# Splitting VectorE's long two-operand operations into instructions of 256 elements, in a graph-network layer

## The chip, the cores and the metric

One NeuronCore of one Trainium2 chip runs the program. The metric is the device time of one execution in microseconds (us); lower is better. The kernel before takes 764.09 us (median of 3 runs, 762.74 to 765.07).

## The reference, cut to what matters

The layer has 50,000 nodes and 25,000 edges (sorted by target node), with rows of 64 floats. Each edge gets an attention score from its type's weight matrix; a softmax over the edges of one target weighs the source rows; then two small products, a leaky ReLU of each, a residual and a layer norm.

```python
proj = jnp.einsum('ni,rio->nro', nfeat, relation_weight)      # 10 relations, 64x64 each
att = jnp.sum(proj[src, etype] * jnp.tanh(proj[dst, etype] + efeat), axis=-1)
ex = jnp.exp(att - segment_max(att, dst)[dst])
a = ex / segment_sum(ex, dst)[dst]
h_nb = segment_sum(nfeat[src] * a[:, None], dst)
out = leaky_relu((nfeat + h_nb) @ res_fc_w.T, 0.01) + leaky_relu(nfeat * h_nb @ res_fc2_w.T, 0.01)
x = layernorm(x + out)
```

Nodes without an incoming edge have h_nb = 0. So the kernel computes every node as if it had none (the "dense" work, 49 tiles of 1,024 nodes), and then overwrites the rows of the nodes that have edges.

## The kernel before, in words

**Edge steps.** Each of the 128 partitions holds 196 consecutive edges (T = 196). A step `s` takes 8 of these columns (COLS = 8, NS = 25 steps, the last of 4 columns). The program of each compute engine is one loop over s = -1 to 28. In it stand the main work of step s (ten relations: VectorE masks, TensorE multiplies), the softmax sums of step s-1 (called e), the head, product and leaky ReLU of step s-2 (called f), the layer norm of step s-3 (called l), and three dense tiles as long as there are any: the last of the 49 is in step 15.

**The rows in and out.** GpSimd (POOL in the profile) issues indirect DMAs only: 384 gathers of x rows into `xsd` (line 441; 128 rows each, indices read from `ends_i`), then 196 scatters of `out_r` into `out` (line 465; indices from `row_i`), and two for the edges that cross partitions: a gather of `es_end` from `hist` ahead of the last 28 scatters, and the very last one. The numbers 0 to 383 below are the gathers, 384 is the first scatter.

**The pace.** So that the gathers don't all come at once, GpSimd waits ahead of its n-th DMA for a point of TensorE's program: as many TensorE instructions (matmuls and weight loads, behind the 12 of the setup) as n*14.6 - 250 for the gathers and n*13.64 - 82 for the scatters. The functions `pe_marks` and `pace` find the semaphore and value for it:

```python
PACE, LEAD, PACE_OUT, LEAD_OUT = 14.6, 250, 13.64, 82
need = [k for k, (_, _, work) in enumerate(marks) if work <= min(n * PACE - LEAD if n < G_MOVES[NS] else n * PACE_OUT - LEAD_OUT, step_end)]
```

A scatter of step s waits also for `fmul_done`, the gather of `es_end` for the store of `hist`.

**What the change touches.** All of it is on VectorE (DVE): `dense_centre` (line 984: zd <- zsd, zd, once for a dense tile), `pair` (lines 1004 and 1005: uw <- h_t, xsd; the sum and the product of head and x), `leaky` (line 1011: l12 in place), `final_add` (1016), `final_add_x` (1021) and `final_centre` (1032), once a step each. All read two tensors from SBUF. `pair_turn` of TensorE and `heads` of ScalarE wait for `uw_done`. Beside these VectorE runs the masks (`xm`, line 912, ten a step, one operand in PSUM), reductions (lines 979, 989, 1026, 1039) and short sums (954).

**The end.** In step 26 VectorE waits at line 1167 for `es_end`; ScalarE's `fmul_done` of the last steps comes behind that.

Of the kernel before, what the change touches and what calls it, by code (L numbers as in the profile page):

```python
# [5 lines left out]
ALU = mybir.AluOpType  # L6
# [6 lines left out]
P = 128  # L13
DMA = 16
COLS = 8
QUAD = 4
BIG = 3.0e38
NONE = 1.0e30
FAR = 1 << 20
SLOPE = 0.01  # L20
EPS = 1e-5

RX = 13
# [11 lines left out]
def wait(eng, sem, value):  # L35

    if value > 0:
        eng.wait_ge(sem, value)


def gnn_resnorm(nc, x, src, dst, eattr, etype, relw, resw, resw2, out):
    N, D = x.shape
# [4 lines left out]
    DR = 512 // D  # L47
# [5 lines left out]
    A0 = (P - 1) // DMA * DMA  # L53
    assert D == 64 and T % QUAD == 0 and (N - (ND - 1) * DB) % DR == 0 and 0 < LASTC < T and T - LASTC <= E

    def cols(s):
        return min(COLS, T - s * COLS)

    def groups(s):
        return cols(s) // QUAD  # L60

    G_BEFORE = [0]
    for s in range(NS):
        G_BEFORE.append(G_BEFORE[-1] + groups(s))
    Q_BEFORE = [2 * n for n in G_BEFORE]
    C_BEFORE = [QUAD * n for n in G_BEFORE]

# [28 lines left out]
    with ExitStack() as ctx:  # L96
# [9 lines left out]
        def sems(name, n):  # L106
# [31 lines left out]
        xsd = sb("xsd", [P, RX, COLS, 2, D])  # L138
# [15 lines left out]
        zsd = sb("zsd", [P, DR])  # L154
# [4 lines left out]
        h_t = sb("h_t", [P, COLS, D])  # L159
        uw = sb("uw", [P, COLS, 2, D])  # L160
        uwT = sb("uwT", [P, 2, 512])
        l12 = sb("l12", [P, COLS, 2, D])
        zf = sb("zf", [P, COLS, D])
        zs = sb("zs", [P, COLS])
        zcf = sb("zcf", [P, 2, COLS, D])
# [37 lines left out]
        zadd_done, zsum_done, zmid_done, dsq_done, dred_done = (  # L203
            sem("zadd_done"), sem("zsum_done"), sem("zmid_done"), sem("dsq_done"), sem("dred_done"))
        sqrt_done, rec_done, dmul_done = sem("sqrt_done"), sem("rec_done"), sem("dmul_done")
        h_done, uw_done, y12_done, pf_done = sem("h_done"), sem("uw_done"), sem("y12_done"), sem("pf_done")
        l_done, z1_done, z2_done, fsum_done, fsub_done = sem("l_done"), sem("z1_done"), sem("z2_done"), sem("fsum_done"), sem("fsub_done")
# [282 lines left out]
        def _(pe):  # L490
# [71 lines left out]
                mm.then_inc(y_done, 1)  # L562

            def pair_turn(f, g):
                pe.wait_ge(uw_done, f + 1)
                wait(pe, tr_out, TR_PAIR[f, g])
                for j in range(QUAD):
                    mm = pe.transpose(tr_ps[:, j * P:(j + 1) * P], uw[:, g * QUAD + j, :, :].rearrange("p k f -> p (k f)"),  # L568
                                      ident[:, :])
                mm.then_inc(tr_in, 1)  # L570
# [13 lines left out]
            for s in range(-1, LAST + 1):  # L584
                main, e, f = 0 <= s < NS, s - 1, s - 2
# [75 lines left out]
        def _(act):  # L661
# [44 lines left out]

            def heads(f, g):
                act.wait_ge(frec_done, f + 1)
                wait(act, uw_done, f)
                for j in range(g * QUAD, (g + 1) * QUAD):  # L710
                    ins = act.activation(h_t[:, j, :], es[:, f % RS, j, :], ACT.Copy, scale=rs[:, f % 2, j:j + 1])  # L711
                ins.then_inc(h_done, 1)
# [34 lines left out]
            for s in range(-1, LAST + 1):  # L747
                e, f, l, o = s - 1, s - 2, s - 3, s - 4
# [79 lines left out]
        def _(v):  # L828
# [152 lines left out]
            def dense_centre(d):  # L981
                v.wait_ge(zsum_done, d + 1)
                z = zd[:, d % RZ, :].rearrange("p (j f) -> p j f", f=D)
                v.scalar_tensor_tensor(z, zsd[:, :].unsqueeze(2).to_broadcast([P, DR, D]), -1.0 / D, z, ALU.mult, ALU.add).then_inc(zmid_done, 1)  # L984

            def dense_sum(d):
                v.wait_ge(dsq_done, d + 1)
# [8 lines left out]
                v.reciprocal(rstd[:, s % 2, :, :], sd[:, s % 2, :, :]).then_inc(rec_done, 1)  # L996

            def pair(f):
                n = cols(f)
                xd = xsd[:, f % RX, 0:n, 1, :]  # L1000
                v.wait_ge(h_done, G_BEFORE[f + 1])
                if f > 0:
                    v.wait_ge(tr_in, TR_PAIR[f - 1, groups(f - 1) - 1] + 1)
                v.tensor_tensor(uw[:, 0:n, 0, :], h_t[:, 0:n, :], xd, ALU.add)
                v.tensor_tensor(uw[:, 0:n, 1, :], h_t[:, 0:n, :], xd, ALU.mult).then_inc(uw_done, 1)

            def leaky(f):
                n = cols(f)
                v.wait_ge(pf_done, Q_BEFORE[f + 1])
                l = l12[:, 0:n, :, :].rearrange("p j k f -> p (j k f)")  # L1010
                v.scalar_tensor_tensor(l, l, SLOPE, l, ALU.mult, ALU.max).then_inc(l_done, 1)

            def final_add(f):
                n = cols(f)
                v.wait_ge(l_done, f + 1)
                v.tensor_tensor(zf[:, 0:n, :], l12[:, 0:n, 0, :], l12[:, 0:n, 1, :], ALU.add).then_inc(z1_done, 1)

            def final_add_x(f):
                n = cols(f)
                v.wait_ge(z1_done, f + 1)  # L1020
                v.tensor_tensor(zf[:, 0:n, :], zf[:, 0:n, :], xsd[:, f % RX, 0:n, 1, :], ALU.add).then_inc(z2_done, 1)

            def final_sum(f):
                n = cols(f)
# [3 lines left out]
            def final_centre(f):  # L1028
                n = cols(f)
                v.wait_ge(fsum_done, f + 1)  # L1030
                wait(v, fmul_done, f - 1)
                v.scalar_tensor_tensor(zcf[:, f % 2, 0:n, :], zs[:, 0:n].unsqueeze(2).to_broadcast([P, n, D]), -1.0 / D,
                                       zf[:, 0:n, :], ALU.mult, ALU.add).then_inc(fsub_done, 1)

            def final_squares(f):
                n = cols(f)
# [5 lines left out]
            for s in range(-1, LAST + 1):  # L1042
                main, e, f, l = 0 <= s < NS, s - 1, s - 2, s - 3
# [169 lines left out]
```

## Time and profile before

| | |
|---|---|
| median of 3 runs | 764.09 us (762.74 to 765.07) |
| profiled execution, span | 764.9 us (its own time is this span, first to last instruction; 0.1% above the median) |
| busy | PE 556.2 (73%), DVE 634.8 (83%), ACT 499.1 (65%), POOL 581.8 (76%) |
| instructions | DVE 1115, POOL 590 |
| chain that ended last | POOL, with line 465 |
| TensorE clock granted | 0.917 in the mean |

POOL's busy time counts each DMA instruction's descriptor work and not the pause behind it, so 76% does not say by itself whether the engine ever waits. DVE's busy share of 83% is a mean over a long stretch of nearly full use and a tail with little to do.

### The profile page before, as it was taken

To read this page: it belongs to the slowest core of one execution; us is meant where nothing else is said; L and a number is where in the kernel's file an instruction comes from. 1 tells how busy PE (TensorE), PEld (TensorE's weight loads), DVE (VectorE), ACT (ScalarE), POOL (GpSimd) and SP (SyncE) were. 2 spreads that over 40 slices of the span, in tenths; PEclk is the share of its full clock that TensorE was granted. 3 is DMA by queue.
4 is the path that set the end of the run, shared out by engine and by line. 5 is a ranking of instruction groups with operands and counts; after the bars stand their busy time and mean duration, and the time that the engine had idled before them with its cause. 6 is when DMAs were issued, how large, how long until landed. Compare 5 with 4: busy or idle time off the path is not lost. (4 is left out here: it accounts for less than half of the span.)

```text
span 764.9 us, 14665 instructions
## 1 busy us (share of the span) xinstructions
PE 556.2 (73%) x3780; PEld 293.9 (38%) x3780; DVE 634.8 (83%) x1115; ACT 499.1 (65%) x1474; POOL 581.8 (76%) x590
## 2 busy tenths in 40 slices
PE   1887888888789788888889887788888788632000
PEld 0652454445345345345345343333333333321000
DVE  1689999999999999999999999999999899742010
ACT  0366677679778779779778777765656446755040
POOL 6777777777777777777777777777777777777776
PEclk9999999999999999999999999999999999755555
DMA  5463435434434434434444332422112221000000
GB/s 134 105 191 81 124 89 144 124 87 145 124 95 137 125 106 126 133 106 117 138 107 115 104 104 73 108 73 75 48 46 74 75 83 44 28 26 17 19 18 16
DMA packets 49457, 70.41 MB, mean 92 GB/s; under 512 B 17450, under 2 KB 20966, under 8 KB 49374
## 3 DMA queue, kind: packets, MB, share of 16 engines
q1 hardware_dynamic: 30750, 52.33, 21.2%
q0 software_dynamic: 18624, 17.16, 10.9%
q8 instruction: 30, 0.49, 0.3%
q14 instruction: 53, 0.43, 0.2%
HBM read 45.61 MB, written 25.78 MB: 93 GB/s over the span
## 5 line engine op out<-in xcount | busy, mean ns | idle before, releaser
L441 POOL DMA_INDIRECT xsd<-in_x,ends_i x384 | 378.2, 985 | 118.0 <-issue 108.6
L543 PE MATMUL t_ps<-xm,w_rel 64*64 64x512 f32 (+1 forms) x1000 | 270.3, 622 | 39.7 <-DVE xm L912 39.2
L912 DVE SCALAR_TENSOR_TENSOR xm<-typ,xT_ps 128x1024 f32<-128x1024 f32 (+1 forms) x250 | 292.4, 1187 | 2.6 <-issue 2.6
L545 PE MATMUL h_ps<-xm,w_rel 64*64 64x512 f32 (+1 forms) x1000 | 270.2, 622 | 0.0
L465 POOL DMA_INDIRECT out<-out_r,row_i x196 | 200.6, 1023 | 59.7 <-issue 55.5
L560 PE MATMUL y_ps<-bd_cat,dT 128*128 128x256 f32 x392 | 97.9, 394 | 17.6 <-DVE zd L974 14.8
L691 ACT ACTIVATE o_t<-zd,rstd 128x64 f32<-128x64 f32 x392 | 98.8, 337 | 14.9 <-DVE rstd L996 14.9
L543 PEld LDWEIGHTS t_ps<-xm,w_rel 64*64 64x64 f32 x1000 | 52.7, 135 | 142.7 <-DVE xm L912 117.4
L578 PE MATMUL s_ps<-bd_both,uwT 128*128 128x128 f32 x392 | 73.4, 313 | 36.6 <-issue 35.9
L578 PEld LDWEIGHTS s_ps<-bd_both,uwT 128*128 128x128 f32 x392 | 54.9, 203 | 115.1 <-issue 95.3
L560 PEld LDWEIGHTS y_ps<-bd_cat,dT 128*128 128x128 f32 x392 | 72.5, 195 | 30.9 <-issue 12.8
L954 DVE SCALAR_TENSOR_TENSOR es<-es,wd,wx 128x64 f32<-128x64 f32 x196 | 55.7, 284 | 11.7 <-ACT wx L704 0.6
L698 ACT ACTIVATE wd<-delta 128x16 f32<-128x16 f32 (+1 forms) x25 | 5.4, 216 | 88.7 <-DVE delta L942 84.4
L568 PE MATMUL tr_ps<-ident,uw 128*128 128x128 f32 x196 | 34.4, 302 | 27.0 <-ACT uwT L718 15.6
L723 ACT COPY l<-s_ps 128x256 f32<-128x256 f32 x98 | 35.2, 359 | 26.9 <-PE s_ps L578 26.9
L545 PEld LDWEIGHTS h_ps<-xm,w_rel 64*64 64x64 f32 x1000 | 52.7, 135 | 0.0
L704 ACT ACTIVATE wx<-xsd,wd 128x64 f32<-128x64 f32 x196 | 52.1, 337 | 0.8
L711 ACT ACTIVATE h_t<-es,rs 128x64 f32<-128x64 f32 x196 | 49.4, 337 | 0.0
L743 ACT ACTIVATE out_r<-zcf,rstd 128x64 f32<-128x64 f32 x196 | 49.2, 333 | 0.1
L568 PEld LDWEIGHTS tr_ps<-ident,uw 128*128 128x128 f32 x196 | 22.3, 150 | 66.8 <-issue 35.0
L974 DVE TENSOR_TENSOR zd<-rd,y_ps 128x512 f32<-128x512 f32 x49 | 33.4, 682 | 9.2 <-ACT rd L677 9.2
L684 ACT ACTIVATE sqd<-zd 128x512 f32<-128x512 f32 x49 | 30.9, 631 | 12.7 <-DVE zd L984 12.6
(143 smaller groups left out, 742.1 us busy)
## 6 DMA issues: line engine op xcount, KB each, us to landing
xsd<-in_x SPq DMA_DIRECT2D x1024, 0.2 KB
x_in<-in_x SPq DMA_DIRECT2D x48, 256.0 KB
typ<-typ_d SPq DMA_DIRECT2D x24, 512.0 KB
out<-o_t SPq DMA_DIRECT2D x48, 256.0 KB
xsd<-in_x,ends_i POOLq DMA_INDIRECT x384
hist<-es SPq DMA_DIRECT2D x24, 256.0 KB, 2.0
ea<-in_edge_attr SPq DMA_DIRECT2D x24, 224.0 KB
out<-out_r,row_i POOLq DMA_INDIRECT x196, 2.1
```

The costliest lines, as they stand in the source:

```text
L441: pool.indirect_dma_start(xsd[:, s % RX, j, side, :], None, x[:, :], bass.IndirectOffsetOnAxis(ap=ends_i[:, side, c:c + 1], axis=0),).then ...
L465: pool.indirect_dma_start(out[:, :], bass.IndirectOffsetOnAxis(ap=row_i[:, c:c + 1], axis=0), out_r[:, s % RW, j, :], None, bounds_check=t ...
L543: pe.matmul(t_ps[h * D:(h + 1) * D, 0:n], w_rel[0:D, r, :], xm[0:D, b, h * n:(h + 1) * n], start=(r == 0), stop=(r == R - 1), skip_group_c ...
L545: mm = pe.matmul(h_ps[(1 - h) * D:(2 - h) * D, 0:n], w_rel[D:P, r, :], xm[D:P, b, (1 - h) * n:(2 - h) * n], start=False, stop=(r == R - 1) ...
L560: mm = pe.matmul(y_ps[:, j * 2 * P:(j + 1) * 2 * P], dT[:, d % 2, j * P:(j + 1) * P], bd_cat.rearrange("p k f -> p (k f)"), start=True, st ...
L568: mm = pe.transpose(tr_ps[:, j * P:(j + 1) * P], uw[:, g * QUAD + j, :, :].rearrange("p k f -> p (k f)"), ident[:, :])
L578: mm = pe.matmul(s_ps[:, YQ + j * P:YQ + (j + 1) * P], uwT[:, q // 2, k * P:(k + 1) * P], bd_both[:, :], start=True, stop=True)
L691: ins = act.activation(o_t[:, d % RO, j * D:(j + 1) * D], zd[:, d % RZ, j * D:(j + 1) * D], ACT.Copy, scale=rstd[:, s % 2, d % 3, j:j + 1])
L704: ins = act.activation(wx[:, j, :], xsd[:, e % RX, j, 0, :], ACT.Copy, scale=wd[:, e % 2, 0, j:j + 1])
L711: ins = act.activation(h_t[:, j, :], es[:, f % RS, j, :], ACT.Copy, scale=rs[:, f % 2, j:j + 1])
L912: v.scalar_tensor_tensor(xm[:, (s * R + r) % RM, 0:n], typ[:, s % RT, 0:n], float(r), xT_ps[:, 0:n], ALU.is_equal, ALU.mult).then_inc(mask ...
L954: v.scalar_tensor_tensor(es[:, e % RS, j, :], old, wd[:, e % 2, 1, j:j + 1], wx[:, j, :], ALU.mult, ALU.add).then_inc(chain_done, 1)
```

## The change

The operations named above are cut along their columns into instructions of 4 columns (256 elements), or 2 columns of `l12` (2 x 2 x 64 = 256 elements). `leaky` becomes four instructions, the others two each. All but `pair` wait and signal as before (the last piece signals). `pair` runs group by group: it waits for `h_done` of 4 columns, adds and multiplies them, and signals `uw_done` once per group; `pair_turn` and `heads` count `uw_done` in groups.

```diff
+HALF = 4
             def pair_turn(f, g):
-                pe.wait_ge(uw_done, f + 1)
+                pe.wait_ge(uw_done, G_BEFORE[f] + g + 1)
...
             def heads(f, g):
-                wait(act, uw_done, f)
+                wait(act, uw_done, G_BEFORE[f])
...
             def dense_centre(d):
-                v.scalar_tensor_tensor(z, zsd[:, :].unsqueeze(2).to_broadcast([P, DR, D]), -1.0 / D, z, ALU.mult, ALU.add).then_inc(zmid_done, 1)
+                for j in range(0, DR, HALF):
+                    ins = v.scalar_tensor_tensor(z[:, j:j + HALF, :], zsd[:, j:j + HALF].unsqueeze(2).to_broadcast([P, HALF, D]), -1.0 / D,
+                                                 z[:, j:j + HALF, :], ALU.mult, ALU.add)
+                ins.then_inc(zmid_done, 1)
...
             def pair(f):
-                n = cols(f)
-                xd = xsd[:, f % RX, 0:n, 1, :]
-                v.wait_ge(h_done, G_BEFORE[f + 1])
                 if f > 0:
                     v.wait_ge(tr_in, TR_PAIR[f - 1, groups(f - 1) - 1] + 1)
-                v.tensor_tensor(uw[:, 0:n, 0, :], h_t[:, 0:n, :], xd, ALU.add)
-                v.tensor_tensor(uw[:, 0:n, 1, :], h_t[:, 0:n, :], xd, ALU.mult).then_inc(uw_done, 1)
+                for g in range(groups(f)):
+                    j = slice(g * QUAD, (g + 1) * QUAD)
+                    xd = xsd[:, f % RX, j, 1, :]
+                    v.wait_ge(h_done, G_BEFORE[f] + g + 1)
+                    v.tensor_tensor(uw[:, j, 0, :], h_t[:, j, :], xd, ALU.add)
+                    v.tensor_tensor(uw[:, j, 1, :], h_t[:, j, :], xd, ALU.mult).then_inc(uw_done, 1)
...
             def leaky(f):
-                l = l12[:, 0:n, :, :].rearrange("p j k f -> p (j k f)")
-                v.scalar_tensor_tensor(l, l, SLOPE, l, ALU.mult, ALU.max).then_inc(l_done, 1)
+                for j in range(0, n, 2):
+                    l = l12[:, j:j + 2, :, :].rearrange("p j k f -> p (j k f)")
+                    ins = v.scalar_tensor_tensor(l, l, SLOPE, l, ALU.mult, ALU.max)
+                ins.then_inc(l_done, 1)
...
             def final_add(f):
-                v.tensor_tensor(zf[:, 0:n, :], l12[:, 0:n, 0, :], l12[:, 0:n, 1, :], ALU.add).then_inc(z1_done, 1)
+                for j in range(0, n, QUAD):
+                    ins = v.tensor_tensor(zf[:, j:j + QUAD, :], l12[:, j:j + QUAD, 0, :], l12[:, j:j + QUAD, 1, :], ALU.add)
+                ins.then_inc(z1_done, 1)
```

`final_add_x` and `final_centre` are cut in the same way as `final_add`.

VectorE's program in the middle of one step, before, from the last small score operation to the first mask behind `pair` (line 942 is `restarts`, 912 `mask`):

```order
L942 TENSOR_TENSOR delta<-delta,start 128x8 [waits sub_done]
L1004 TENSOR_TENSOR uw<-h_t,xsd 128x8x64 [waits tr_in,h_done]
L1005 TENSOR_TENSOR uw<-h_t,xsd 128x8x64
L984 SCALAR_TENSOR_TENSOR zd<-zsd,zd 128x512 [waits zsum_done]
L912 SCALAR_TENSOR_TENSOR xm<-typ,xT_ps 128x1024 [waits quad_done] x2
```

The same place in the changed program (its line numbers are up to 13 higher):

```order
L943 TENSOR_TENSOR delta<-delta,start 128x8 [waits sub_done]
L1009 TENSOR_TENSOR uw<-h_t,xsd 128x4x64 [waits h_done,tr_in]
L1010 TENSOR_TENSOR uw<-h_t,xsd 128x4x64
L1009 TENSOR_TENSOR uw<-h_t,xsd 128x4x64 [waits h_done]
L1010 TENSOR_TENSOR uw<-h_t,xsd 128x4x64
L986 SCALAR_TENSOR_TENSOR zd<-zsd,zd 128x256 [waits zsum_done]
L986 SCALAR_TENSOR_TENSOR zd<-zsd,zd 128x256
L913 SCALAR_TENSOR_TENSOR xm<-typ,xT_ps 128x1024 [waits quad_done] x2
```

Three instructions between the score work and the next mask have become six; the mask keeps its place behind them, and the first half of `uw` is whole after two of them.

VectorE's program at the end of the same step, before:

```order
L969 RECIPROCAL rs<-s_all 128x8 [waits h_done,den_done]
L1011 SCALAR_TENSOR_TENSOR l<-l 128x1024 [waits pf_done]
L1016 TENSOR_TENSOR zf<-l 128x512 [waits l_done]
L919 TENSOR_TENSOR prod<-t_ps,g_t 128x512 [waits att_done,tanh_done]
L1021 TENSOR_TENSOR zf<-zf,xsd 128x512 [waits z1_done]
```

And in the changed program:

```order
L970 RECIPROCAL rs<-s_all 128x8 [waits h_done,den_done]
L1017 SCALAR_TENSOR_TENSOR l<-l 128x256 [waits pf_done]
L1017 SCALAR_TENSOR_TENSOR l<-l 128x256 x3
L1024 TENSOR_TENSOR zf<-l 128x256 [waits l_done]
L1024 TENSOR_TENSOR zf<-l 128x256
L920 TENSOR_TENSOR prod<-t_ps,g_t 128x512 [waits att_done,tanh_done]
L1031 TENSOR_TENSOR zf<-zf,xsd 128x256 [waits z1_done]
L1031 TENSOR_TENSOR zf<-zf,xsd 128x256
```

Nothing changes its place; three instructions with two SBUF operands have become eight, and `product`, which TensorE waits for, stands behind six of them instead of two. The programs of TensorE, ScalarE, GpSimd and SyncE keep their instructions and their order.

## Rows read from the trace of the kernel before

**Rows 1.** Chain that ended last, in order of time: start us, us, what.
```profile
758.85 0.30 issue
759.15 0.97 POOL out L465
```

**Rows 2.** Waits of POOL: waited for, us in total, times, longest.
```profile
POOL xsd L441 <- issue: 108.6, 356, 0.3
POOL out L465 <- issue: 55.5, 182, 0.3
POOL xsd L441 <- PE h_ps L545: 5.5, 18, 0.3
```

**Rows 3.** Lines 441 and 465: duration ns min/median/max, then first and last start.
```profile
L441 POOL DMA_INDIRECT xsd<-in_x,ends_i x384: 940/944/2074, 3.6 to 497.6; - x192
L465 POOL DMA_INDIRECT out<-out_r,row_i x196: 971/972/1947, 498.8 to 759.2; - x196
```

**Rows 4.** Page, groups: the same two lines, busy us, mean ns.
```profile
L441 POOL DMA_INDIRECT xsd<-in_x,ends_i x384 | 378.2, 985 | 118.0 <-issue 108.6
L465 POOL DMA_INDIRECT out<-out_r,row_i x196 | 200.6, 1023 | 59.7 <-issue 55.5
```

**Rows 5.** Timeline of DVE, middle of a step: start us, us, what.
```profile
311.99 0.69 DVE L1004 TENSOR_TENSOR uw<-h_t,xsd 128x512 f32<-128x512 f32 x1
312.59 0.69 DVE L1005 TENSOR_TENSOR uw<-h_t,xsd 128x512 f32<-128x512 f32 x1
313.19 0.69 DVE L984 SCALAR_TENSOR_TENSOR zd<-zsd,zd 128x512 f32<-128x512 f32 x1
```

**Rows 6.** Timeline of POOL beside it.
```profile
312.63 1.47 POOL L441 DMA_INDIRECT xsd<-in_x,ends_i  x1 [0.30 <-issue]
314.40 0.94 POOL L441 DMA_INDIRECT xsd<-in_x,ends_i  x1 [0.30 <-issue]
```

**Rows 7.** Timeline of DVE and of POOL, end of a step without dense work.
```profile
556.11 1.23 DVE L1011 SCALAR_TENSOR_TENSOR l<-l 128x1024 f32<-128x1024 f32 x1 [0.34 <-ACT l L723]
...
556.85 1.33 POOL L465 DMA_INDIRECT out<-out_r,row_i  x1 [0.30 <-PE h_ps L545]
```

**Rows 8.** Timeline of POOL and of DVE, the longest gather.
```profile
478.92 2.07 POOL L441 DMA_INDIRECT xsd<-in_x,ends_i  x1 [0.30 <-PE h_ps L545]
...
478.86 0.69 DVE L1004 TENSOR_TENSOR uw<-h_t,xsd 128x512 f32<-128x512 f32 x1
479.47 0.69 DVE L1005 TENSOR_TENSOR uw<-h_t,xsd 128x512 f32<-128x512 f32 x1
```

**Rows 9.** Timeline of DVE, the step of 4 columns: operations of 256 elements.
```profile
685.83 0.42 DVE L1004 TENSOR_TENSOR uw<-h_t,xsd 128x256 f32<-128x256 f32 x1
686.17 0.42 DVE L1005 TENSOR_TENSOR uw<-h_t,xsd 128x256 f32<-128x256 f32 x1
686.51 0.68 DVE L1026 TENSOR_REDUCE zs<-zf 128x8 f32<-128x512 f32 x1
```

**Rows 10.** Groups of DVE by form, 200 to 600 us: busy, mean ns, idle before.
```profile
L912 DVE SCALAR_TENSOR_TENSOR xm<-typ,xT_ps 128x1024 f32<-128x1024 f32 x156 | 185.9, 1209 | 0.0
...
L1011 DVE SCALAR_TENSOR_TENSOR l<-l 128x1024 f32<-128x1024 f32 x16 | 19.2, 1200 | 3.3 <-ACT l L723 3.3
```

**Rows 11.** Windows from the start: us, then busy and instructions (x) by engine.
```profile
0.00:482.60 482.60, 394.82 (x2654) 215.57 (x2654) 445.94 (x764) 355.82 (x1068) 367.05 (x380) 0.99 0.42 117
```

**Rows 12.** Timeline of POOL, the last gathers and the first scatter.
```profile
493.84 0.94 POOL L441 DMA_INDIRECT xsd<-in_x,ends_i  x1 [0.30 <-issue]
...
498.83 1.00 POOL L465 DMA_INDIRECT out<-out_r,row_i  x1 [0.30 <-issue]
```

**Rows 13.** Groups of POOL in 500:620, 620:700 and 700:765.
```profile
L465 POOL DMA_INDIRECT out<-out_r,row_i x92 | 93.0, 1011 | 28.1 <-issue 24.4 <-PE h_ps L545 3.0 <-PE s_ps L578 0.6
L465 POOL DMA_INDIRECT out<-out_r,row_i x58 | 62.4, 1076 | 17.7 <-issue 17.1 <-PE s_ps L578 0.3 <-PE h_ps L545 0.3
L465 POOL DMA_INDIRECT out<-out_r,row_i x46 | 45.1, 980 | 14.0 <-issue 14.0
```

**Rows 14.** Timeline of DVE, the wait for es_end.
```profile
725.49 0.28 DVE L1167 SCALAR_TENSOR_TENSOR before<-es_end,fix,xT_ps 128x64 f32<-128x64 f32 x1 [26.55 <-DMA es_end<-hist,fix_i]
```

More of the change, by code:

```diff
@@ L1020, in final_add_x @@
                 v.wait_ge(z1_done, f + 1)
-                v.tensor_tensor(zf[:, 0:n, :], zf[:, 0:n, :], xsd[:, f % RX, 0:n, 1, :], ALU.add).then_inc(z2_done, 1)
+                for j in range(0, n, QUAD):
+                    ins = v.tensor_tensor(zf[:, j:j + QUAD, :], zf[:, j:j + QUAD, :], xsd[:, f % RX, j:j + QUAD, 1, :], ALU.add)
+                ins.then_inc(z2_done, 1)
             def final_sum(f):
@@ L1031, in final_centre @@
                 wait(v, fmul_done, f - 1)
-                v.scalar_tensor_tensor(zcf[:, f % 2, 0:n, :], zs[:, 0:n].unsqueeze(2).to_broadcast([P, n, D]), -1.0 / D,
-                                       zf[:, 0:n, :], ALU.mult, ALU.add).then_inc(fsub_done, 1)
+                for j in range(0, n, QUAD):
+                    ins = v.scalar_tensor_tensor(zcf[:, f % 2, j:j + QUAD, :], zs[:, j:j + QUAD].unsqueeze(2).to_broadcast([P, QUAD, D]),
+                                                 -1.0 / D, zf[:, j:j + QUAD, :], ALU.mult, ALU.add)
+                ins.then_inc(fsub_done, 1)
             def final_squares(f):
```

## Prediction

> **What bounds the kernel now.** I read the chain that ended last first. It is GpSimd from end to end, in the pattern 0.30 us of issue and 0.97 us of an indirect DMA [rows 1]. The list of GpSimd's waits says that this holds for the whole span: 356 gathers and 182 scatters began 0.3 us behind the one before them with nothing to wait for, and where TensorE is named it is the same 0.3 us at most [rows 2]. So the pace is not felt today, and the time is a sum over one engine: 582 DMAs, each with a pause of 0.30 us. What can shorten it is the DMA instruction itself. Its median is 944 ns for a gather and 972 ns for a scatter, with longest ones of 2074 and 1947 [rows 3], but the means are 985 and 1023 [rows 4]. The difference is time lost on the chain: 384 x 0.041 = 15.7 us in the gathers and 196 x 0.051 = 10.0 us in the scatters, 25.7 us in all.
>
> **What lengthens a DMA instruction.** I laid the two timelines side by side. The gather of 312.63 took 1.47 us, 0.53 more than its median [rows 6]. It began while L1005 ran (312.59, 0.69 us, so to 313.28) [rows 5], and 0.53 is the time from its start to that end, less 0.12. The scatter of 556.85 is 0.36 too long, and L1011 ran from 556.11 to 557.34: 0.49 less 0.13 [rows 7]. So a DMA instruction that starts inside a VectorE operation with two SBUF operands stands until this operation ends. The masks, with one operand in PSUM, are far more numerous (L912, 156 in 400 us [rows 10]), and I found no gather held by one. The other lengthened instructions that I laid beside VectorE's timeline fit in the same way, most of them with L1005 and L1011. As a rule a GpSimd instruction gets in between two such operations in a row: that of rows 6 did, with L984 right behind L1005. Not always: the one of 478.92 started in L1004, and was held through L1005 as well, to 480.16 [rows 8].
>
> The Trainium skill, SBUF — State Buffer, section "Who interferes with whom", describes this: VectorE and GpSimd share one port pair, taken as an exclusive lock for a whole instruction, and a VectorE instruction with two SBUF inputs contends with a GpSimd one that reads SBUF. The trace agrees (0.53 us). The same section infers that a tensor_tensor does not hold back descriptor generation; L1005 is a TENSOR_TENSOR and does. What that would make of the time is the second rival.
>
> **What the pieces give.** Held at most for the rest of one operation, a DMA loses up to 0.69 - 0.13 = 0.56 us behind 512 elements and up to 1.1 behind 1024; a piece lasts 0.42 us in the record [rows 9], so at most 0.42 - 0.13 = 0.29 can be lost, on average half of that, 0.15. The chance to be hit stays, as the pieces cover the same stretch and a little more. In the scatters without dense work today's loss is 92 x (1011 - 972) = 3.6 us, then 58 x (1076 - 972) = 6.0 us, then 46 x 8 ns = 0.4 us [rows 13]. The first part is ten delays like that of rows 7, each of which would be near 0.15 on average; the second, at 104 ns for each of 58, has to hold some much longer ones, which would be at most 0.29. I take 3.6 to 1.8, 6.0 to 2.4, and 0.4 to 0.2: 4.4 us lost, 5.6 us won. If each delay were placed badly (0.29), the gain is 3; if well, 8.
>
> For the gathers the same halving would give about 8 of 15.7 us, if nothing else stopped them. The pace does.
>
> **What the pieces cost.** A step gets 8 more instructions (pair 2, leaky 3, the other three 1 each), and each of the 49 dense tiles 1: 25 x 8 + 49, about 245. The price of one more can be read: two operations of 512 elements start 0.60 us apart (311.99, 312.59, 313.19 [rows 5]), two of 256 elements 0.34 (685.83, 686.17, 686.51 [rows 9]): 2 x 0.34 - 0.60 is 0.07 to 0.08, I take 0.07. Nothing hides it on VectorE: it has no idle time ahead of its masks in 400 us, and 3.3 us ahead of sixteen L1011 [rows 10], which can swallow a little of it. So masks, and TensorE's program behind them, come 0.07 x 11 = 0.77 us later in each step with dense work, and the delays add up from step to step.
>
> This matters through the pace. GpSimd's n-th gather may not start before TensorE has done n x 14.6 - 250 instructions. For n = 380 that is 5298. The window to 482.60 has 2654 + 2654 = 5308, less 12 of the setup 5296 [rows 11], so the point is reached at about 482.6; the gather was issued at 493.84 [rows 12]. The slack is 11.2 us. By then the changed VectorE has run some 14 steps x 8 and 49 dense pieces more: 161 x 0.07 = 11.3 us. A GpSimd that ran 8 us ahead would need 19; so in the second half of the gathers GpSimd runs into the pace and follows TensorE. The first scatter (498.83 before [rows 12]) then comes at 498.83 - 11.2 + 11.3, so where it was; with some of VectorE's waits swallowed, 1 us sooner. The gain of the gathers is given back.
>
> The scatters have a laxer pace: for the first, n = 384, 384 x 13.64 - 82 = 5156 instructions, 200 less than the gathers' rule would ask, some 18 us of TensorE's work at the 5308 in 482.6 us [rows 11]. They start free and stay so, as 13.64 a DMA is less than TensorE does in 1.28 us.
>
> **The end.** VectorE waits 26.55 us for `es_end` [rows 14]; the added work up to there is at most 245 x 0.07 = 17 us, and GpSimd comes 6.5 us sooner: 3 us are left, and behind it GpSimd has 28 scatters to issue before it needs the last `fmul_done`. Nothing on the chain. `pair`'s signal by half gives TensorE its first `uw` 0.6 us earlier, but its next masks are behind the whole of `pair`; I count it at nothing, and if TensorE lost that cover, it is worth 0.6 us a step at most to the pace.
>
> **Sum.** 764.9 of the profiled execution - 1.0 (gathers) - 5.6 (scatters) = 758.3; the median of the runs is 0.8 us under the profiled one, so 757.5.
>
> **Rivals.**
> 1. *The gathers gain too.* If the pieces cost less to the path than 0.07 each (VectorE's waits swallow more, or pieces overlap better), the slack lasts longer. With 0.02 an instruction, 3 us, the pace is not reached: 764.1 - 8 - 5.6 = 750.5; halfway between, 753. For: VectorE's 3.3 us of waiting. Against: no idle time ahead of the masks. Chance 0.13.
> 2. *The pieces don't do what they are cut for.* GpSimd is held through a row of pieces, as it was at 478.92 [rows 8], or what holds it is not the single operation. Then the losses stay at 25.7 us, and the gathers end at the pace or where they did: 764.1 to 765. Against: rows 6. Chance 0.14. By what the Trainium skill's SBUF page infers the tensor_tensor pieces belong here as well.
> 3. *Slower: dear instructions.* If the pieces don't overlap, one more costs 2 x 0.42 - 0.69 = 0.15 us [rows 5, 9]. Then TensorE is 161 x 0.15 = 24 us late at n = 380, and the first scatter 13 us later: 764.1 + 13 - 5.6 = 771.5; the end's wait is then used up too. It decides from the point at which the lateness passes 11.2 + 5.6 + 2.3 = 19 us, 0.12 us an instruction. Against it are the starts in rows 9. Chance 0.08.
> 4. *Bad phase.* DMA and steps keep step with each other, so delays repeat; with new lengths they could repeat at the worst place, and save 3 us or less: 761.8 to 763. Chance 0.10.
>
> The Trainium skill, VectorE: DVE Perf Modes, advises against such a cut: its section on the TRN2 errata wants tiles of 512 elements or more, and its formula for fp32 (N + 151 cycles) would make one more instruction cost 0.157 us, an estimate that leads to the third rival, some 772. The starts 0.34 us apart in rows 9 speak for half of it.
>
> **Numbers.** The forecast as told, 754.5 to 761.5, has 0.55; the rivals 0.45. About 0.3% (2.3 us) is what a measurement here can tell from no change, so faster means under 761.8. Faster: 0.55 + 0.13 and a little of rival 4, 0.70. Same: rivals 2 and most of 4, 0.21. Slower: 0.09. The range leaves out the third rival and the free gathers: 752 to 765.5.
>
> **What would show it.** The median of the two DMA lines unchanged, the mean of line 465 near 995, no scatter much over 1.3 us except where pieces chain; L1005 and L1011's successors 0.33 us apart; GpSimd's list of waits now with several us under TensorE's lines in 250 to 498 us; the first scatter at 497 to 499 us; the wait for `es_end` down to 3 to 10 us. The prediction is wrong if the first scatter has moved by more than 3 us, or if the mean of line 465 has not fallen.

## The result, and the profile after

The changed kernel takes 772.66 us (median of 4 runs, 771.89 to 773.72) against 764.58 us before: 8.1 us slower, ratio 1.0104 [1.0085, 1.0123] (small, but clear of noise). The forecast was 757.5. In fourteen of the eighteen experiments (marked * below, and called stalled) the kernel before itself took 914 to 926 us, with idle stretches of a microsecond and more between instructions on all engines, so their ratios are against the kernel before as it ran beside them, and their times are compared with no others.

GpSimd is still the chain. These are the groups of its two lines in the profile after (busy us, mean ns, idle before), the counterpart of [rows 4]:

```profile
L442 POOL DMA_INDIRECT xsd<-in_x,ends_i x384 | 383.1, 998 | 118.0 <-issue 105.2
L466 POOL DMA_INDIRECT out<-out_r,row_i x196 | 198.9, 1015 | 61.5 <-issue 55.8
```

The gathers have become longer (985 to 998 ns in the mean, 4.9 us in all) where they should have become shorter until the pace stopped them; the scatters have won 8 ns each, 1.7 us, of the 5.6 forecast. The list of GpSimd's waits has a row that [rows 2] did not have:

```profile
POOL out L466 <- DMA out<-o_t: 2.1, 1, 2.1
```

And this is the timeline of GpSimd at the end of its gathers, beside [rows 12]:

```profile
501.18 0.94 POOL L442 DMA_INDIRECT xsd<-in_x,ends_i  x1 [0.31 <-issue]
502.43 1.04 POOL L442 DMA_INDIRECT xsd<-in_x,ends_i  x1 [0.30 <-issue]
505.55 1.00 POOL L466 DMA_INDIRECT out<-out_r,row_i  x1 [2.09 <-DMA out<-o_t]
```

The first scatter comes at 505.55 instead of 498.83, 6.7 us later; from there to the end it is 764.9 - 498.8 = 266.1 us before and 769.9 - 505.6 = 264.3 after. So the profiled execution is 5.0 us longer: 6.7 lost up to the first scatter, 1.8 won behind it. The medians differ by 3 us more than the two spans, most likely because the profiled execution of before was a long one: a run's time is 1.7 to 2.3 us over its span wherever both are on record (the changed kernel: 771.98 and 769.9), so I estimate that the span of 764.9 belongs to a time near 767. Beside k1 eleven runs of the kernel before had spans of 760.2 to 763.5.

The 6.7 us have two sources. The last gather ends at 503.47 instead of 498.53, so after the usual 0.30 us the first scatter would have come at 503.77: 4.9 us are the gathers' own. Another 1.8 us are the wait.

What the scatters wait for stands between the two loops of the GpSimd program: `pool.wait_ge(o_stored[k], o_need(k))`. A scatter overwrites rows that the dense work has written, so the last store of dense rows must have landed. The DMA queue's timeline, before and then after:

```profile
488.34 5.96 SPq L377 DMA_DIRECT2D xsd<-in_x  x16
494.35 0.73 SPq L311 DMA_DIRECT2D out<-o_t  x2
```

```profile
496.33 5.95 SPq L378 DMA_DIRECT2D xsd<-in_x  x16
502.33 0.73 SPq L312 DMA_DIRECT2D out<-o_t  x2
```

Step 16 of the queue's program reaches the store behind 16 row loads of 0.37 us each. All of it is 8.0 us later than before: VectorE's lateness, handed on. By the trace's records of the transfers the last bytes landed at 496.9 before and at 504.65 after, 7.7 us later, and in every profile where the gathers were done by then the first scatter came 0.9 us behind that landing. Before it came 1.9 us behind: the slack was 1.0 us. So either source alone would have moved the first scatter: the gathers by 4.9 us, the store by 6.7.

### The profile page after: what moved, and what is told of

Same layout as the page of the kernel before. It is cut to its first block and busy times, and to the rows that moved or that the text cites. A ratio compares the mean times of both kernels' runs of the same rounds, so it can differ in the third digit from the quotient of the medians.

```text
span 769.9 us, 14907 instructions
## 1 busy us (share of the span) xinstructions
PE 564.0 (73%) x3780; PEld 300.6 (39%) x3780; DVE 650.1 (84%) x1357; ACT 499.1 (65%) x1474; POOL 585.1 (76%) x590
## 3 DMA queue, kind: packets, MB, share of 16 engines
q1 hardware_dynamic: 30750, 52.33, 20.4%
## 5 line engine op out<-in xcount | busy, mean ns | idle before, releaser
L442 POOL DMA_INDIRECT xsd<-in_x,ends_i x384 | 383.1, 998 | 118.0 <-issue 105.2
L544 PE MATMUL t_ps<-xm,w_rel 64*64 64x512 f32 (+1 forms) x1000 | 274.5, 639 | 37.7 <-DVE xm L913 37.4
L546 PE MATMUL h_ps<-xm,w_rel 64*64 64x512 f32 (+1 forms) x1000 | 274.3, 639 | 0.0
L466 POOL DMA_INDIRECT out<-out_r,row_i x196 | 198.9, 1015 | 61.5 <-issue 55.8
L561 PE MATMUL y_ps<-bd_cat,dT 128*128 128x256 f32 x392 | 103.5, 411 | 23.3 <-DVE zd L975 21.3
L544 PEld LDWEIGHTS t_ps<-xm,w_rel 64*64 64x64 f32 x1000 | 56.5, 139 | 141.9 <-DVE xm L913 102.2
L561 PEld LDWEIGHTS y_ps<-bd_cat,dT 128*128 128x128 f32 x392 | 75.6, 203 | 37.7 <-issue 18.1
L546 PEld LDWEIGHTS h_ps<-xm,w_rel 64*64 64x64 f32 x1000 | 56.6, 140 | 0.0
L678 ACT ACTIVATE rd<-y_ps 128x512 f32<-128x512 f32 x49 | 28.8, 589 | 22.5 <-PE y_ps L561 18.6
```

The lines of the kernel that those rows point to most:

```text
L442: pool.indirect_dma_start(xsd[:, s % RX, j, side, :], None, x[:, :], bass.IndirectOffsetOnAxis(ap=ends_i[:, side, c:c + 1], axis=0),).then ...
L466: pool.indirect_dma_start(out[:, :], bass.IndirectOffsetOnAxis(ap=row_i[:, c:c + 1], axis=0), out_r[:, s % RW, j, :], None, bounds_check=t ...
L544: pe.matmul(t_ps[h * D:(h + 1) * D, 0:n], w_rel[0:D, r, :], xm[0:D, b, h * n:(h + 1) * n], start=(r == 0), stop=(r == R - 1), skip_group_c ...
L546: mm = pe.matmul(h_ps[(1 - h) * D:(2 - h) * D, 0:n], w_rel[D:P, r, :], xm[D:P, b, (1 - h) * n:(2 - h) * n], start=False, stop=(r == R - 1) ...
L561: mm = pe.matmul(y_ps[:, j * 2 * P:(j + 1) * 2 * P], dT[:, d % 2, j * P:(j + 1) * P], bd_cat.rearrange("p k f -> p (k f)"), start=True, st ...
```

## The experiments

Theory 1: VectorE's lateness, through the last dense store, delays the first scatter. Theory 2: the pieces of `pair` stand in a row and hold a DMA instruction longer than a whole operation did. "Holds" are sums that I made from the timelines: each DMA instruction's excess over its median (944 or 972 ns), if over 12 ns, from 60 us on, put to the VectorE operation running at its start. They are 24.8 us before and 28.3 after.

**The two engines keep step.** Theory 1 as it stands has only one path for the lateness, and the same timelines show a second. From one `uw` to the next VectorE's step is, in the change, the difference of these two starts, 28.92 us (VectorE; lines between left out):

```profile
288.02 0.42 DVE L1009 TENSOR_TENSOR uw<-h_t,xsd 128x256 f32<-128x256 f32 x1
316.94 0.42 DVE L1009 TENSOR_TENSOR uw<-h_t,xsd 128x256 f32<-128x256 f32 x1
```

Before, a typical step is 28.2. In nearly every step GpSimd starts 22 gathers. Unheld, 22 gathers with their pauses last 22 x (0.944 + 0.30) = 27.4 us, and what the step lasts beyond that is time in which they are held. Medians of the 12 steps between 100 and 450 us, by the same sums as the holds:

| kernel | VectorE's step, us | gathers in it | held in it, us |
|---|---|---|---|
| before | 28.20 | 22 | 0.73 |
| e5 (memsets) | 28.26 | 22 | 0.74 |
| e6 (`leaky` in pieces) | 28.43 | 22 | 0.91 |
| j1 (small reductions) | 28.77 | 22 | 1.30 |
| k1 (early stores) | 28.91 | 22 | 1.40 |
| the change | 28.92 | 22 | 1.44 |

What the step grows by, the held time grows by: 0.72 and 0.71 us in the change, 0.57 and 0.57 in j1, where nothing is cut. Behind the gathers it is the same with 16 scatters (medians from 500 to 640 us): 0.72 us held in a step of 21.15 before, 1.06 in one of 21.49 in the change. So while a step holds the same number of DMAs, lateness is paid in held DMAs at once, and small pieces only choose where. (This is a reading of the rows: an unheld DMA would come earlier in the next step, and after a few steps be caught again.) The 11 pieces of a step with three dense tiles cost 0.72 us, 0.066 each. TensorE's mean granted clock was lower too, 0.96 for 0.98 between 60 and 480 us, but VectorE is busy for 407 and 408 of these 420 us, and the price of the pieces alone accounts for its longer step.

**Theory 2 in the change's own profile.** VectorE, then GpSimd:

```profile
288.69 0.42 DVE L1009 TENSOR_TENSOR uw<-h_t,xsd 128x256 f32<-128x256 f32 x1
289.03 0.42 DVE L1010 TENSOR_TENSOR uw<-h_t,xsd 128x256 f32<-128x256 f32 x1
289.36 0.75 DVE L986 SCALAR_TENSOR_TENSOR zd<-zsd,zd 128x256 f32<-128x256 f32 x2
```

```profile
288.99 1.94 POOL L442 DMA_INDIRECT xsd<-in_x,ends_i  x1 [0.30 <-issue]
```

The gather of 288.99 began in one of pair's pieces and stood until the last piece of the whole run was over: 289.36 + 0.75 - 288.99 - 0.13 = 0.99 us. Near the start a gather that began in the third of the four pieces stood through the fourth and the two of `zd` behind them (VectorE, then GpSimd; the first of the four, at 85.09, is not shown):

```profile
85.43 0.42 DVE L1010 TENSOR_TENSOR uw<-h_t,xsd 128x256 f32<-128x256 f32 x1
85.77 0.42 DVE L1009 TENSOR_TENSOR uw<-h_t,xsd 128x256 f32<-128x256 f32 x1
86.10 0.42 DVE L1010 TENSOR_TENSOR uw<-h_t,xsd 128x256 f32<-128x256 f32 x1
86.44 0.76 DVE L986 SCALAR_TENSOR_TENSOR zd<-zsd,zd 128x256 f32<-128x256 f32 x2
```

```profile
85.92 2.09 POOL L442 DMA_INDIRECT xsd<-in_x,ends_i  x1 [0.30 <-issue]
```

2.09 - 0.94 is 1.15 us, and 86.44 + 0.76 - 85.92 - 0.13 is the same. This repeats in most steps: 19 of the 24 DMAs caught in `uw` were held for over 0.6 us (3 of 24 before), 19.6 us against 11.7. They are not 19 independent cases: eleven were caught within 25 ns of the same point of the third piece, as the two engines kept step. In the stalled runs of the same pieces, where they do so less, it was 7 of 19 and 4 of 15 (e2, f2). None of the 71 caught in the pieces of `leaky`, `final_add`, `dense_centre` or `final_centre` was. Of these 71, 36 had another piece directly behind them (21 of `leaky`, 14 of `final_add`, 1 of `dense_centre`); the others were the last of their run and say nothing about runs. There the pieces did what was expected of them, as here (VectorE, then GpSimd):

```profile
307.61 0.76 DVE L1024 TENSOR_TENSOR zf<-l 128x256 f32<-128x256 f32 x2
```

```profile
307.69 1.17 POOL L442 DMA_INDIRECT xsd<-in_x,ends_i  x1 [0.30 <-issue]
```

The hold of 0.22 us ends with the first of the two pieces (0.42 long), though the second follows at once. Holds in `leaky` went from 9.9 to 1.4 us.

**e1\*, e5: small memsets, nothing cut.** The kernel before, and behind each operation one line for each piece that the change adds:

```diff
+                for _ in range(groups(f) - 1):
+                    k = next(idle_n)
+                    v.memset(idle_t[:, k:k + 1], 0.0)
```

> The kernel before, whole operations, with one tiny VectorE instruction (a memset of one column of a tile that nobody reads) added for each piece that the change adds: VectorE is late as in the change, and no operation is cut. Theory 1 (lateness: the first scatter waits for the last store of the dense rows, which is late with VectorE): the first scatter at 505 to 506 us instead of 498.8, GpSimd waits some us for out<-o_t, and the span is 6 to 8 us over that of before, ratio about 1.009. Theory 2 (the held gathers alone: runs of pieces in pair hold a DMA for 0.99 us): no such holds here, first scatter within 1 us of 498.8, ratio 1.000.

Measured: 1.0004 [0.9977, 1.0030].

> The same kernel as e1 (whole operations, one tiny VectorE instruction added for each added piece), since in the runs around e1 the kernel before itself took 916 us. If the kernel before is at 764 again: theory 1 (lateness through the stores of the dense rows) expects the first scatter at 505 to 506 us, a wait for out<-o_t, and a ratio of about 1.009; theory 2 (held gathers alone) 1.000 and the first scatter within 1 us of 498.8.

Measured: 763.52 us, ratio 0.9952 [0.9935, 0.9969]. It did not test lateness, since a memset costs VectorE almost nothing; the first scatter came at 498.11, behind a wait of 0.55 us for the stores. VectorE's timeline in e5:

```profile
301.68 1.18 DVE L1019 SCALAR_TENSOR_TENSOR l<-l 128x1024 f32<-128x1024 f32 x1
302.81 0.07 DVE L1022 MEMSET idle_t<- 128x1 f32 x3
302.89 0.69 DVE L1027 TENSOR_TENSOR zf<-l 128x512 f32<-128x512 f32 x1
```

The add behind `leaky` starts 1.21 us after `leaky` does, with the three memsets as without them; three pieces cost 0.21. The queue issued the last stores at 494.71, only 0.36 us later than before. The ratio says little more: beside e5 and e6 the kernel before had its highest median of those not stalled (767.00), and 764 is what it took elsewhere.

**f1\*, g1\*, h1\*, i2\*, j1: the same with a small reduction**, which costs nearly what a piece costs (in j1 0.07 us each behind `pair`, 0.03 behind `leaky`):

```diff
-                    v.memset(idle_t[:, k:k + 1], 0.0)
+                    v.tensor_reduce(idle_t[:, k:k + 1], ident[:, 0:8], AX.X, ALU.add)
```

> The kernel before with one small VectorE reduction (8 elements to 1, one SBUF input, into a column that nobody reads) added for each piece that the change adds. The memset of e5 took only 8 ns of VectorE's time, so e5 had no lateness; small operations of 8 elements start 75 ns apart, the price of a piece. Theory 1 (lateness): the steps of VectorE take 29.0 us instead of 28.3, the last dense store lands at 504 to 506, GpSimd waits 1 to 7 us for out<-o_t, and the span is 5 to 8 us over before: ratio about 1.008 against a before of 765. Theory 2 (held gathers alone): within 0.3% of before.

> The same kernel as f1 (lateness alone, no pieces), since the kernel before itself took 926 us around f1. Where before is near 765: theory 1 expects VectorE's steps of 29.0 us, the last dense store at 504 to 506, a wait for out<-o_t, and 5 to 8 us over before (ratio about 1.008). Theory 2 (held gathers alone): within 0.3% of before.

> The same kernel as g1 (VectorE late by one small reduction for each added piece, nothing cut), for a chip on which the kernel before takes 764 to 767 us. Theory 1 (lateness through the last dense store): step 29.0 us, last store landed at 504 to 506, a wait for out<-o_t, 5 to 8 us over before. Theory 2 (held gathers alone): within 0.3% of before.

> The same kernel as h1 (lateness alone, nothing cut), for a time when the kernel before takes 764 to 767 us. Theory 1: store landed at 504 to 506, a wait for out<-o_t, 5 to 8 us over before. Theory 2 (held gathers alone): within 0.3% of before.

> Lateness alone, nothing cut, as i2. In all profiles so far the first scatter came 0.9 us behind the landing of the last dense store, or behind the gathers where these were later. For a kernel before of 764 to 767 us: theory 1: store landed at 503 to 505, first scatter 0.9 us behind it, 4 to 8 us over before. Theory 2: first scatter at 498 to 499, within 0.3% of before.

Measured: f1 1.0043 [0.9999, 1.0087], g1 0.9988 [0.9947, 1.0028], h1 1.0028 [1.0003, 1.0053], i2 1.0010 [0.9981, 1.0039], all stalled; and j1, the one that tells: 774.16 us against 763.89, ratio 1.0136 [1.0116, 1.0156]. VectorE's timeline in j1 has the small instruction take its place for 0.07 to 0.08 us (301.70 to 301.78):

```profile
301.11 0.68 DVE L986 SCALAR_TENSOR_TENSOR zd<-zsd,zd 128x512 f32<-128x512 f32 x1
301.70 0.15 DVE L989 TENSOR_REDUCE idle_t<-ident 128x1 f32<-128x8 f32 x1
301.78 0.68 DVE L1049 SCALAR_TENSOR_TENSOR zcf<-zs,zf 128x512 f32<-128x512 f32 x1
```

and GpSimd's:

```profile
503.45 0.94 POOL L443 DMA_INDIRECT xsd<-in_x,ends_i  x1 [0.30 <-issue]
506.28 1.00 POOL L467 DMA_INDIRECT out<-out_r,row_i  x1 [1.89 <-DMA out<-o_t]
```

By the records of the transfers the last store landed at 505.4, 8.5 us later than before; the first scatter came 7.5 us later, and the profiled span is 8.0 us over before. Lateness alone, without one piece, costs more than the change does (10.3 us by the medians, where up to 8 were expected). That lateness makes the loss is shown. That it does so through the store alone is not: the gathers ended at 504.4 and would have put the first scatter at 504.7, so 5.9 of the 7.5 us are the gathers' own (4.4 in their duration, 1.4 in the pauses before them), mostly by the second path above, and 1.6 are the wait. The holds are 30.5 us, of which 17.6 in `leaky`. Two of the 8.5 us of lateness were there at the first `uw` already (87.2 us, before 85.2, change 85.1) and stay unexplained, so j1 shows the kind of the loss better than its size.

**e6: leaky alone in pieces.** The diff is that of `leaky` above.

> The kernel before with leaky alone in four pieces (3 more instructions a step, 3 us of lateness by the last dense store). Theory 2: leaky held DMA instructions for 9.9 us in all in the profile of before; in pieces 1 to 3 us, and pair's operations, whole, hold as before. Theory 1: the first scatter comes 3 us later than in before in spite of it, at 501 to 502, behind a wait for out<-o_t. Together, with about 4 us won in the scatters: ratio 0.998 to 1.000; by theory 2 alone 0.990.

Measured: 765.53 us against 767.00, ratio 0.998 [0.9965, 0.9995]. The last gathers and the first scatter:

```profile
497.14 0.95 POOL L441 DMA_INDIRECT xsd<-in_x,ends_i  x1 [0.30 <-issue]
499.36 1.00 POOL L465 DMA_INDIRECT out<-out_r,row_i  x1 [1.26 <-DMA out<-o_t]
```

The wait for the stores is there again, after only 1.5 us of lateness in the landing (498.45 for 496.9). And the holds moved: 9.9 us in `leaky` became 1.6, but 22 DMAs were caught in `final_add`, whole here and right behind it, for 9.7 us. A hold sets the time of the next DMA, so DMAs and steps repeat together; to cut one operation sends them into its neighbour, and the held time of a step is still what the step leaves (0.91 us). Holds fell by 3.8 us in all.

**e3\*, f3\*, g2\*, i1\*: the change with pair whole.**

```diff
-                for g in range(groups(f)):
-                    j = slice(g * QUAD, (g + 1) * QUAD)
-                    xd = xsd[:, f % RX, j, 1, :]
-                    v.wait_ge(h_done, G_BEFORE[f] + g + 1)
...
+                v.wait_ge(h_done, G_BEFORE[f + 1])
+                v.tensor_tensor(uw[:, 0:n, 0, :], h_t[:, 0:n, :], xd, ALU.add)
+                v.tensor_tensor(uw[:, 0:n, 1, :], h_t[:, 0:n, :], xd, ALU.mult).then_inc(uw_done, 1)
```

> The changed kernel with pair as it was (two operations of 512 elements, signalled once a step); all else is in pieces. Theory 2: the holds of 0.99 us in pair are gone (at most 0.55 each), the lengthening of all DMA instructions falls from 31 us to 12 to 15, and GpSimd reaches the end of the gathers some 10 us sooner. Theory 1: the first scatter does not come sooner by that, since VectorE is only 2 us less late: it comes at 503 to 504 us behind a wait for out<-o_t of 8 us or more; the scatters win 3 to 4 us. Ratio about 1.001 by both together, 1.007 by theory 1 if the scatters win nothing, 0.990 by theory 2 alone.

> The changed kernel with pair as it was, as e3. Theory 2: no run of pair's pieces, so no holds of 0.99 us; holds fall from 31 us to 12 to 17 in all. Theory 1: the first scatter nonetheless waits for out<-o_t, until 503 to 504. Together: span 764 to 766, GpSimd idle 5 us or more ahead of the first scatter. By theory 2 alone: the first scatter at 492, span 755.

> The same kernel as f3 (the change with pair whole). Where before is near 765: holds fall from 31 us to 12 to 17, the last dense store lands at 502 to 504 and GpSimd waits 5 us or more for it, span 764 to 766 if both theories hold; by theory 2 alone the first scatter at 492 and a span of 755; by theory 1 alone, with holds as in the change behind the first scatter, 768.

> The same kernel as g2 (the change with pair whole), for a time when the kernel before takes 764 to 767 us. Theory 2 (runs of pieces in pair hold a DMA): holds fall from 31 us to 12 to 17 in all. Theory 1 (lateness through the last dense store): the store lands at 502 to 504 and GpSimd waits 5 us or more for it. Span 764 to 766 if both hold; by theory 2 alone 755; by theory 1 alone 768.

Measured: 1.0029 [1.0002, 1.0055], 1.0007 [0.9979, 1.0035], 1.0008 [0.9983, 1.0033], 1.0009 [0.9977, 1.0041]. All four were stalled, so the span expected was not tested; that holds would fall to 12 to 17 us in all was met (11.7 to 13.2).

**e4\*, f4\*: pair alone in pieces.** The diff is that of `pair` and its two waits above.

> The kernel before with pair alone in pieces by half. Theory 2: pair's run of four pieces and the dense operation behind it (whole here, 512) holds DMAs for about 1 us in most steps, and leaky (whole) holds others up to 1 us: the lengthening of the DMA instructions is 30 us or more, and the last gather is the late one: first scatter at 503 to 506 us, with no wait for the stores; ratio 1.008 to 1.012. Theory 1 (lateness alone): pair adds 2 x 0.07 us a step, 2 us by the last dense store; ratio 1.002.

> The kernel before with pair alone in pieces by half, as e4. Theory 2: holds of about 1 us in most steps at pair, and up to 1 us at leaky: 30 us or more in all, first scatter at 503 to 507 without a wait for the stores, span 770 or more. Theory 1 (lateness alone): 2 us of lateness, span 766.

Measured: 1.0015 [0.9985, 1.0044] and 1.0010 [0.9980, 1.0040], and holds of 19.5 and 20.4 us where 30 were expected. So what the pieces of `pair` alone cost where nothing is stalled is not known.

What the stalled runs do tell is holds at mixed phases, since the stalls scatter the DMAs over VectorE's program. In all, in us: nothing cut 16.2, 22.6, 20.3, 19.0, 20.5 (e1, f1, g1, h1, i2); all cut but pair 13.2, 12.1, 11.7, 11.9 (e3, f3, g2, i1); everything cut 15.6, 12.5 (e2, f2); pair alone cut 19.5, 20.4 (e4, f4). In `uw` alone 4.0 to 6.7 whole (e1, f1, g1, h1, i2), and in pieces 9.3, 5.4, 6.6, 6.4 (e2, f2, e4, f4). So cutting the others takes about 8 of 20 us, and cutting `pair` takes nothing. This is the gain that the prediction reckoned with; it appears where DMAs and steps don't repeat together. The group of the gathers in g2 and in g1:

```profile
L442 POOL DMA_INDIRECT xsd<-in_x,ends_i x384 | 370.4, 965 | 225.6 <-issue 93.4 <-remote 79.6 <-PE h_ps L546 26.8
```

```profile
L443 POOL DMA_INDIRECT xsd<-in_x,ends_i x384 | 375.5, 978 | 220.3 <-issue 87.3 <-remote 64.7 <-PE h_ps L547 40.2
```

**e2\*, f2\*, k1: the change with the last stores ahead of the row loads.**

```diff
...
+                ending = ND - 1 in tiles(s - 1)[0:2]
+                if ending:
+                    for n in tiles(s - 2)[2:3] + tiles(s - 1)[0:2]:
+                        store_o(n)
                 rows_at((s - 1) * PER_STEP)
```

(and their old places left out in that step).

> The changed kernel, with the stores of the last two dense tiles moved ahead of the row loads in the DMA queue's program of step 16 (they are issued some 5 us earlier). Theory 1: the wait for out<-o_t ahead of the first scatter (2.1 us in the profile of the change) is gone, and the first scatter comes at once behind the gathers, at 503 to 504 us; 2 us are won. Theory 2 (held gathers alone): in the end the gathers' own 22 us of holds stay, so the rest of the loss stays too. Both together: ratio 1.007 to 1.008. If lateness were the whole loss, the gathers would end near 499 and the ratio would be 1.000.

> The changed kernel with the stores of the last two dense tiles ahead of the row loads in step 16, as e2. Theory 1: no wait for out<-o_t ahead of the first scatter; the first scatter at 503 to 504 (the end of the gathers with 22 us of holds), 2 us won of the change's 769.9. If the stores were the only thing: 499 and 763. Span 767 to 768 by both theories together.

> The changed kernel with the stores of the last two dense tiles ahead of the row loads in step 16, as e2 and f2. Where the kernel before takes 764 to 767 us: theory 1 expects the last store landed at 500 to 502, the first scatter at once behind the gathers (503.5 in the change), with no wait for out<-o_t, and 2 us less than the change's 8 us over before: ratio 1.007 to 1.009. Theory 2 (held gathers alone): the same end of the gathers and no gain over the change, 1.010.

Measured: e2 0.9966 [0.9940, 0.9993], f2 0.9953 [0.9926, 0.9980], the only two stalled kernels besides m1 that beat their before clear of noise; GpSimd's wait for the stores was 4.4 and 8.3 us in them and 3.2 in m1, 9.0 to 20.1 in the other stalled ones. k1: 766.20 us against 764.25, ratio 1.0032 [1.0015, 1.0050]; two thirds of the change's loss are gone. In its profile the queue has issued the last store by 499.1 and the scatters follow the gathers with the usual pause. The queue, then GpSimd:

```profile
491.90 7.20 SPq L312 DMA_DIRECT2D out<-o_t  x3
500.20 4.73 SPq L378 DMA_DIRECT2D xsd<-in_x  x12
```

```profile
501.64 1.08 POOL L446 DMA_INDIRECT xsd<-in_x,ends_i  x1 [0.30 <-issue]
503.02 1.22 POOL L470 DMA_INDIRECT out<-out_r,row_i  x1 [0.30 <-issue]
```

The first scatter moved by 2.5 us, as expected. The other 4.4 us of the span's 6.9 (769.9 to 763.0) are in the scatters:

```profile
L470 POOL DMA_INDIRECT out<-out_r,row_i x196 | 194.5, 992 | 59.8 <-issue 58.0 <-PE h_ps L550 1.2 <-PE s_ps L583 0.6
```

992 ns in the mean for 1015: of the holds over 0.6 us the scatters have 1 here and 6 in the change, though the pieces are the same. That was not expected. From 550 us on VectorE's steps last 23 us in k1 with 18 scatters each, of which some 0.26 us are held, and not 21.5 with 16 and 1.06; why they do was not looked into. So of k1's gain only the 2.5 us are the store's, and the rest is where the two engines fell against each other.

**m1\*: k1 with pair whole.** The diff is that of e3 on top of k1's.

> The changed kernel with pair whole again and the last dense stores moved forward, both edits that the theories ask for. Theory 1: the last store lands at 498 to 500 (2 us less late than in k1), and is the later of the two; theory 2: without pair's runs the gathers end at 492 to 496. First scatter at 499 to 501, 2 to 4 us ahead of k1, and scatters with 3 to 5 us of holds: span 759 to 762, ratio to before 0.996 to 1.000 where before takes 764.

Measured: 0.9956 [0.9928, 0.9985], with 13.2 us of holds and a wait of 3.2 us for the stores. The ratio is a little under the 0.996 to 1.000 expected, which were for a kernel before of 764 us; that it would beat that is not shown.

## Why the prediction was wrong

**The first scatter (the step that failed).** The prediction had it "where it was" or 1 us sooner, and it came 6.7 us later, at 505.55. Two terms were wrong.

The first is the gathers' own time. The prediction halved the time that they are held and let the pace eat the gain; lateness of VectorE counted only against the pace. In the profiles GpSimd keeps step with VectorE, and the 0.72 us that a step grew by came back as 0.71 us of held gathers in it. The gathers' busy time rose from 378.2 to 383.1 us, and they ended 4.9 us later.

The second is a wait that the prediction put at nothing by leaving it out. It priced the lateness against the pace and against `es_end`, and not against the third wait of GpSimd's program, the stores of the dense rows. It had 1.0 us of slack, and the landing is 7.7 us later. The wait did not show in [rows 2] because the gathers finished a little later than the landing; a wait that is met is in no list. Beyond the gathers' lateness it costs 1.8 us; with the gathers on time it would have cost 6.7.

j1 shows that lateness without pieces makes such a loss (both terms together), and k1 that the store's part goes when the store does: 2.5 us back, while its gathers still end at 502.7.

**The price of a piece was right.** Pieces start 0.33 to 0.34 us apart (288.69, 289.03, 289.36), and a step of 11 of them is 0.72 us longer, against 0.77 forecast. By the forecast's point of the pace 0.07 us each add up to 11.3 us; the stores of step 16 came 8.0 us late. The first `uw` is not late at all (85.1 us, before 85.2), so the pieces up to there were swallowed, more than the forecast allowed for.

**The pace was not reached.** By the forecast's own sum it needed gathers that win 8 us, and they lost 5. That "the chance to be hit stays" is not so where DMAs come at the same point of each step: it is decided once and repeats. The fourth rival said this ("DMA and steps keep step with each other") and bounded the harm at a saving of 3 us or less; that the step's length sets the held time it did not say. For `pair` the halving failed as well. The prediction knew the case [rows 8], called it an exception and gave it to rival 2; its counter-example, the gather of [rows 6], was caught in L1005, with no second operation of `pair` behind it. Of the six DMAs caught in L1004 before, two stood through L1005 too. In pieces, at this phase, it became the rule, 19 of 24.

**The scatters** won 1.7 us (busy 200.6 to 198.9) of 5.6; six holds of 0.95 to 0.97 us, all in `pair`, ate the rest. In k1, where only one of them occurred, the same pieces won 6.1, so the 5.6 was within reach, by the phase.

**The end.** The wait for `es_end` fell from 26.55 to 22.2 us, as GpSimd came 5 us later and not 6.5 sooner; nothing on the chain, as said.

**Spans and medians.** The prediction took the span for the profiled execution's own time. Its sum does not suffer, since 764.1 - 6.6 is 757.5 all the same, but the reader should know that of the 8.1 us between the medians the two profiles show 5.0.

The third rival gave 771.5, near the measured time, by a dear instruction; the price was not the cause, and that its number fits is luck. It had lateness handed on to the first scatter, which is what counted, but through the pace.

**Open.** Why runs of `uw` pieces often hold a DMA to their end and runs of the others let it in. In the change all eighteen caught within 60 ns of a `uw` piece's start, or 298 ns and more behind it, were held on. Of the six caught at 145 to 210 ns four were let in (one by the last piece of its run) and two held on (85.92, for 1.15 us, and 510.72, for 0.43). The point in the piece doesn't explain it: in the stalled e2 and f2 eight DMAs caught at 290 ns and later of a `uw` piece, with another behind it, were held for 0 to 0.31 us. A wait on each piece, or `dense_centre` moved behind the next mask, would tell more; neither was tried. How large the gain of m1 would be at 764 us is open too. That the length of the step sets the held time is read from the six kernels of the table; no run changed the number of DMAs in a step, or GpSimd's own period, to test it.

## What to carry to other kernels

Before an engine that is "not the bound" is made slower, list every wait in the bound engine's program, the met ones too, and read for each how long ago it was met; these slacks are the price list, not the list of waits in the profile. When the bound engine loses time to another one, count its instructions in each step of that other. If the number is the same in every step, the lost time is what the step leaves over, and making the other engine's instructions shorter while its step gets longer gains nothing. When an operation is cut to let another engine in, look at what stands directly before and behind it: in this kernel runs of such operations often counted as one. And where two engines keep step, a difference of 3 us can be phase alone: test lateness with instructions of the right price, and repeat.

## What the runs showed of the hardware

A VectorE operation of 256 elements with two SBUF inputs that caught a DMA instruction held it until 0.13 us before the operation's recorded end; with a recorded length of 0.42 us and starts 0.335 apart, I estimate that this leaves gaps of some 45 ns between pieces. In the change a waiting DMA got in behind all 36 pieces of `l`, `zf` and `zd` that had caught one and had another piece behind them, and behind 3 of 23 of pair's. By the Trainium skill, SBUF — State Buffer, section "Who interferes with whom", a tensor_tensor takes the shared read interface, and only its effect on descriptor generation is inferred to be none; here TENSOR_TENSOR pieces held indirect DMAs for 0.22 us (the gather of 307.69) to 0.97 (the scatter of 553.17, with no other kind of operation beside them).

Two memsets of one column behind `pair` moved VectorE's next operation by 0.02 us (1.20 to 1.22 us behind pair's start), three behind `leaky` by nothing; two reductions of 8 elements behind `pair` moved it by 0.14, three behind `leaky` by 0.09. The kernel before, unchanged, spread from 763.64 to 769.55 us over the 13 runs beside e5 and e6, as wide as most of the effects here.
